# Q, K and V of a linear attention by seven products of halves in place of eight

## The chip, the cores and the metric

The kernel runs on one core of a Trainium2 chip. A core has TensorE (PE in the profile) for matrix products, VectorE (DVE), ScalarE (ACT) and GpSimd (POOL) for elementwise work, and SyncE (SP), which here only issues DMAs. Their common memory is SBUF, with 128 partitions; TensorE writes its sums to PSUM, eight banks of 128 x 512 numbers in 32 bits. The metric is the time of one execution on the device in microseconds (us), as the median of three runs.

## The reference

The input `x` is 4 blocks of 512 tokens with 512 features. Three layers follow, each with a layer norm in front and added to `x`: an FFN, an attention without softmax, and the same FFN again.

```python
def ffn(x, w_gate_up, w_proj):                 # w: ternary per group of 64
    gate, up = split(x @ ternary(w_gate_up).T) # 512 -> 2 x 2048
    h = silu(gate) * up
    return rms_norm(h) @ ternary(w_proj).T     # 2048 -> 512

def attention(x, w_qkv, w_proj, b_proj):       # 16 heads of 32
    q, k, v = relu(x @ wq.T), relu(x @ wk.T), x @ wv.T
    vk = [v, 1].T @ k                          # per head, 33 x 32
    out = vk @ q.T
    out = out[:-1] / (out[-1] + 1e-15)
    return out @ w_proj.T + b_proj

x = x + 0.5 * ffn(layernorm(x))
x = x + attention(layernorm(x))
x = x + 0.5 * ffn(layernorm(x))
```

## The kernel before

The tokens are cut into 16 tiles of 128 (tile i, quarter q; block b has four tiles). First the ternary FFN weights are made; then the tiles pass through the first FFN (`ffn_tile`, i from 0 to 15), the four blocks through attention, and the tiles again through the second FFN (i from 16 to 31). Each engine has its own instruction list in an order written out by hand, and semaphores are the only tie between the lists: `dve.wait_ge(rs_done, n)` holds VectorE's whole queue until the count is reached. An engine never takes a later instruction first.

An activation goes into a product as two numbers of 16 bits, a high and a low part (`x_high` is ScalarE's copy to 16 bits, `x_low` is VectorE's remainder). SyncE then turns both with a DMA transpose (`turn_x`, `turn_h`), since a product wants features on the partitions. Attention weights are cut the same way: w x = high high + high low + low high, three products for each 128 features.

In a tile of the FFN, TensorE makes for each quarter q eight products into a gate bank and eight into an up bank (`gate_up`, L1190), with two banks of each, so that quarter q+2 waits until quarter q has been read. ScalarE reads gate (`silu_gate`), VectorE multiplies with up (`hidden`, L884), ScalarE squares for the norm (`square`), and the tile before is scaled and cut (`h_high`, `h_low`, L897). After the four quarters `project` makes the 32 products of an older tile (`BEHIND` names it: 13 has tile 11, 14 has 12, 15 has 13, and 12 has both 9 and 10). `h_turned(i)` and `h_halves(i)` lie in a ring of eight slots, at i-2 and i-1.

In tiles 12 to 15 the sixteen units of attention weights (128 rows of w_qkv or w_proj) are cut, one at each quarter: `cut_high` on ScalarE (L757), its remainder on VectorE (L1074), `turn_unit` and `load_unit` on SyncE (L461 to L468). Two buffers (`aw_raw`) take turns.

In a block of attention `qkv(b, u)` (L1318) makes two banks for each u from 0 to 5: K for u 0 and 1, V for 2 and 3, Q for 4 and 5, with twelve products of 512 columns to a bank. ScalarE empties one of the two banks and VectorE the other. `keys_values` sums over tokens. Then for b > 0 come `project_attention(b-1, 0)`, `sums_by_queries(b)` (the denominators), `project_attention(b-1, 1..3)`, and `values_by_queries(b)`. Between the two by-queries steps ScalarE takes the logarithm and the exponential (L795, L799) as a guess of the inverse, and VectorE checks and mends it (`check_guess` L1094, `mend_guess` L1101); the checks also free the banks for the values. `att_out(b-1, t)` (L921, L924) adds a projection to `x` and so empties one of the two `proj_ps` banks; a projection waits until the one two uses before it has been taken. The layer norm and the turns of the next block run beside all this.

## Time and profile before

| | us |
|---|---|
| three runs | 882.1, 881.82, 881.25; median 881.82 |
| span of the profiled execution | 880.1 |

The profiled execution's own time is its span from the first to the last instruction; the runs' median is 1.7 us longer. In the profile TensorE is busy 98% of the span, VectorE 54%, ScalarE 45%, GpSimd 8%. Tiles 12 to 15 of the first FFN go from 261 to 351 us, attention from 351 to 535.5. A row of the timeline or the chain gives the start in us, then the length in us, the engine, the line and how many instructions were merged; what ended the idle time ahead of it stands in brackets. A product of 512 columns is shown with 379 ns, but they overlap: the next begins 216 ns later.

### The profile page before, as it was taken

Reading aid. Unit: us, or ns where it says so; the run is one execution under the profiler, and the core shown is the slowest. Engines: PE = TensorE matmul, PEld = TensorE weight load, DVE = VectorE, ACT = ScalarE, POOL = GpSimd, SP = SyncE. Lnnn points to the kernel's source line nnn. Section 1 sums busy time; section 2 is a strip of 40 time slices with the busy share of each in tenths; the row PEclk is TensorE's granted clock in tenths of the full one; section 3 lists DMA queues with packets and bytes.
Section 4 is the critical chain, followed back from the end, with each engine's and each line's share of the span. In section 5 each row is a group of like instructions: output and inputs, shape, how many; then the busy total and the mean of one; then the engine's idle time right before and its main releaser. Section 6 shows DMA issues by size and latency. Waiting matters only on the chain.

```text
span 880.1 us, 12730 instructions
## 1 busy us (share of the span) xinstructions
PE 863.7 (98%) x4836; PEld 404.0 (46%) x4902; DVE 478.1 (54%) x911; ACT 399.1 (45%) x762; POOL 71.3 (8%) x106
## 2 busy tenths in 40 slices
PE   6999999999999999999999999999999999999998
PEld 5544444444444444444444444444444444444445
DVE  7999997833335445518393938544334444333232
ACT  7976667555344445233333325343444434433331
POOL 2211001200000000100000000000000100000000
DMA  9998409985446677520203010063343334332336
GB/s 255 188 185 116 72 1 179 210 187 143 84 68 138 120 173 154 82 57 1 50 1 43 7 36 14 12 118 75 73 72 72 72 72 73 73 72 60 60 66 138
DMA packets 234829, 80.79 MB, mean 92 GB/s; under 512 B 221201, under 2 KB 224017, under 8 KB 234769
## 3 DMA queue, kind: packets, MB, share of 16 engines
q1 hardware_dynamic: 226944, 67.92, 40.8%
q0 software_dynamic: 3872, 4.72, 3.9%
q10 hardware_dynamic: 3952, 7.34, 2.5%
q8 instruction: 39, 0.64, 0.3%
q14 instruction: 22, 0.17, 0.1%
HBM read 25.43 MB, written 4.19 MB: 34 GB/s over the span
## 4 chain that ended last, share of the span: by engine, by line
PE 93%; DVE 3%; DMA 1%; issue 1%; ACT 1%; SPq 0%; DVEq 0%; ACTq 0%
PE proj_ps L1214 23%; PE gate_ps L1200 22%; PE up_ps L1200 22%; PE sum_ps L1337 5%; PE proj_ps L1237 5%; PE up_ps L1337 5%; PE gate_ps L1337 5%; PE proj_ps L1200 3%; PE gate_ps L1247 1%; DMA xs<-xn 1%; PE sum_ps L1186 1%; PE proj_ps L1350 1%; DMA xs<-in_L_attn_x_dram 1%; DVE stats L858 0%; PE gate_ps L1225 0%
## 5 line engine op out<-in xcount | busy, mean ns | idle before, releaser
L1214 PE MATMUL proj_ps<-down_w,slots 128*128 128x512 bf16 x909 | 202.7, 379 | 1.1 <-issue 0.2
L1200 PE MATMUL gate_ps<-gu_w,xT 128*128 128x512 bf16 (+1 forms) x878 | 199.8, 367 | 0.9
L1200 PE MATMUL up_ps<-gu_w,xT 128*128 128x512 bf16 (+1 forms) x878 | 199.7, 367 | 0.9
L884 DVE SCALAR_TENSOR_TENSOR slots<-up_ps,silu 128x512 f32<-128x512 f32 x117 | 80.9, 691 | 172.1 <-PE up_ps L1200 151.1
L631 ACT ACTIVATE silu<-gate_ps 128x512 f32<-128x512 f32 x117 | 69.0, 590 | 165.2 <-PE gate_ps L1200 165.1
L1214 PEld LDWEIGHTS proj_ps<-down_w,slots 128*128 128x128 f16 x928 | 90.7, 98 | 110.1 <-DVE xs L906 0.8
L1200 PEld LDWEIGHTS gate_ps<-gu_w,xT 128*128 128x128 f16 x896 | 85.5, 98 | 99.0
L1200 PEld LDWEIGHTS up_ps<-gu_w,xT 128*128 128x128 f16 x896 | 85.3, 98 | 98.2
L641 ACT ACTIVATE o_buf<-slots 128x512 f32<-128x512 f32 x128 | 80.4, 628 | 100.3 <-DVE slots L884 99.3
L897 DVE SCALAR_TENSOR_TENSOR slots<-slots,inv 128x512 f16<-128x512 f32 x124 | 91.1, 743 | 1.2 <-ACT slots L652 1.1
L906 DVE SCALAR_TENSOR_TENSOR xs<-proj_ps,xs 128x512 f32<-128x512 f32 x31 | 21.4, 691 | 126.3 <-PE proj_ps L1214 126.3
L652 ACT ACTIVATE slots<-slots,inv 128x512 f16<-128x512 f32 x124 | 86.5, 711 | 7.7 <-POOL inv L559 4.2
L554 POOL TENSOR_TENSOR rs<-ve,neg_half 128x1 f32<-128x1 f32 x48 | 39.7, 826 | 393.4 <-DVE ve L860 393.3
L559 POOL TENSOR_TENSOR inv<-ms,neg_half 128x1 f32<-128x1 f32 x32 | 18.8, 588 | 328.3 <-DVE ms L892 321.2
L1237 PE MATMUL proj_ps<-att_w,slots 128*128 128x512 f16 x192 | 42.6, 379 | 0.0
L618 ACT ACTIVATE xn<-lnx 128x512 f16<-128x512 f32 x44 | 27.6, 628 | 30.4 <-DVE lnx L867 30.3
L694 ACT ACTIVATE att_w<-sum_ps 128x1024 bf16<-128x1024 f32 x24 | 24.7, 1028 | 22.2 <-PE sum_ps L1186 21.7
L858 DVE BATCH_NORM_STATS2 stats<-xs 128x6 f32<-128x512 f32 x48 | 32.9, 685 | 2.1 <-DMA xs<-in_L_attn_x_dram 2.1
L1337 PE MATMUL up_ps<-att_w,xT 128*128 128x512 f16 x144 | 33.0, 379 | 0.0
L1337 PE MATMUL gate_ps<-att_w,xT 128*128 128x512 f16 x144 | 33.0, 379 | 0.0
L877 DVE TENSOR_TENSOR xn<-lnx,xn 128x512 f16<-128x512 f32 x44 | 30.1, 685 | 0.3
L1237 PEld LDWEIGHTS proj_ps<-att_w,slots 128*128 128x128 f16 x192 | 18.6, 98 | 24.4 <-DVE xs L921 2.5
(138 smaller groups left out, 773.4 us busy)
## 6 DMA issues: line engine op xcount, KB each, us to landing
out_dram<-xs SPq DMA_DIRECT2D x15, 256.0 KB, 2.4
xs<-in_L_attn_x_dram SPq DMA_DIRECT2D x3, 1024.0 KB, 7.3
aw_raw<-in_L_attn_w_qkv_dram ACTq DMA_DIRECT2D x12, 256.0 KB, 2.8
slots<-in_L_ffn_w_gate_up_dram ACTq DMA_DIRECT2D x5, 512.0 KB, 6.9
aw_raw<-in_L_attn_w_qkv_dram SPq DMA_DIRECT2D x8, 256.0 KB, 3.0
aw_raw<-in_L_ffn_w_gate_up_dram POOLq DMA_DIRECT2D x4, 256.0 KB, 4.9
aw_raw<-in_L_ffn_w_proj_dram POOLq DMA_DIRECT2D x4, 256.0 KB, 5.1
aw_raw<-in_L_attn_w_proj_dram ACTq DMA_DIRECT2D x4, 256.0 KB, 2.7
```

The lines of the kernel that those rows point to most:

```text
L554: nc.gpsimd.tensor_tensor(rs[:, t:t + 1], ve[:, t:t + 1], neg_half[:, :], ALU.pow).then_inc(rs_done, 1)
L631: nc.scalar.activation(silu_rows(j), bank(gate_ps, j), ACT.Silu, scale=gu_out(i))\
L641: nc.scalar.activation(junk, h_rows(i, q), ACT.Square, accum_out=ssq[:, i % 8, q:q + 1])\
L652: nc.scalar.activation(h_halves(i)[:, 0, q * 512:(q + 1) * 512], h_rows(i, q), ACT.Copy, scale=inv[:, i % 8:i % 8 + 1]).then_inc(hi_done, 1)
L858: step.done(nc.vector.bn_stats(out=stats[:, t, :], in_=x_tile(m % 4, t)))
L877: nc.vector.tensor_tensor(xn[:, t, 1, :], lnx[:, t % 2, :], xn[:, t, 0, :], ALU.subtract)\
L884: nc.vector.scalar_tensor_tensor(out=h_rows(i, q), in0=bank(up_ps, j), scalar=gu_out(i), in1=silu_rows(j), op0=ALU.mult, op1=ALU.mult).the ...
L897: nc.vector.scalar_tensor_tensor(out=h_halves(i)[:, 1, q * 512:(q + 1) * 512], in0=h_rows(i, q), scalar=inv[:, i % 8:i % 8 + 1], in1=h_hal ...
L1200: mm = nc.tensor.matmul(bank(ps, j)[:, first:first + width], xT(m)[:, t, r, k, :], gu_w[:, k, c:c + width], start=(k + r == 0), stop=(k == ...
L1214: mm = nc.tensor.matmul(proj_ps[:, use % 2, :], h_turned(i)[:, r, j, :], down_w[:, j, :], start=(r + j == 0), stop=(r == 1 and j == HC - 1))
L1237: mm = nc.tensor.matmul(proj_ps[:, use % 2, :], out_turned(b)[:, k, r, t * P:(t + 1) * P], att5[:, s, k, 12:16, :].rearrange("p u m -> p ( ...
L1337: mm = nc.tensor.matmul(dst, lhs, rhs, start=(m == 0), stop=(m == len(terms) - 1))
```

## The change

The product of an activation matrix and a weight matrix, each cut into halves along both sides, takes eight products of halves. The change takes seven (Strassen's scheme in Winograd's form), with sums of halves made on both sides.

- Weights: a pair of units (`pair_units(n)`, six pairs: four of K and V, two of Q) is loaded into `w_forms`, and `pair_sums` (VectorE, four steps of 256 columns) makes seven forms of 256 columns there, 1792 in all. `pair_high` (ScalarE) and `pair_low` (VectorE) cut them in two steps of 896 columns each, and `turn_pair` turns both parts. There is one `w_forms`: `load_pair(n+1)` waits for `pair_low(n)`. This runs in tiles 12 to 14. The four units of w_proj follow in tile 15 and block 0.
- Activations: for tiles s and s+2 of a block `spread` (ScalarE) writes the normed rows, `forms_sums` (VectorE, four steps of 256), `forms_high` and `forms_low` (two steps of 896 each) and `turn_forms` follow. For block 0 they run in tiles 13 to 15, for the others one block ahead.
- Products: `product(b, s, p)` for s = 0, 1 makes K and V of two pairs of tiles with six products of 512 columns, for s = 2 Q with twelve of 256. Their order is the table `PRODUCTS`. Three banks gather each s; `part` copies what stands in a bank midway, `summed` adds such a copy to another bank, `positive` takes the relu.
- Places: K, V, Q and the copies lie where the gate and up weights lay. `keep_weights` writes these to DRAM in tiles 8 to 11 (GpSimd's queue, four times 1 MB), and `bring_weights` reads them back from the end of `keys_values(3)` on.
- Order: the outputs of block b-1 (`output`, `output_low`) now run in block b; `att_out(b-1, 1)` stands behind the four `check_guess`; the four projections of block 3 stand behind quarter 1 of tile 16, not behind quarter 3.

SyncE's queue from the turn of tile 12's hidden rows on (`slots<-slots`, 16 squares) into tile 14, before. `att_w<-aw_hl` and `att_w<-bias` are turns of one unit, `aw_raw<-in_L_attn_w_qkv_dram` its load.

```order
L455 DMA_TRANSPOSE slots<-slots 128x16x128 [waits hi_done,hT_here1,hT_here0]
L455 DMA_TRANSPOSE slots<-slots 128x16x128 [waits lo_done]
L435 DMA_TRANSPOSE xT<-xn 128x8x128 [waits up_done,xn_done]
L468 DMA_TRANSPOSE att_w<-aw_hl 128x8x128 [waits awlo_done]
L464 DMA aw_raw<-in_L_attn_w_qkv_dram 128x512
L468 DMA_TRANSPOSE att_w<-bias 128x8x128 [waits awlo_done]
L464 DMA aw_raw<-in_L_attn_w_qkv_dram 128x512
L468 DMA_TRANSPOSE att_w<-aw_hl 128x8x128 [waits awlo_done]
L464 DMA aw_raw<-in_L_attn_w_proj_dram 128x512
```

The same place after. `att_w<-slots` with 14 squares is `turn_pair`, `aw<-in_L_attn_w_qkv_dram` is `load_pair`, in eight pieces of 32 rows where Q is loaded.

```order
L567 DMA_TRANSPOSE slots<-slots 128x16x128 [waits hi_done,hT_here1,hT_here0]
L567 DMA_TRANSPOSE slots<-slots 128x16x128 [waits lo_done]
L589 DMA_TRANSPOSE att_w<-slots 128x14x128 [waits whigh_done]
L589 DMA_TRANSPOSE att_w<-slots 128x14x128 [waits wlow_done]
L579 DMA aw<-in_L_attn_w_qkv_dram 32x512 [waits wlow_done]
L579 DMA aw<-in_L_attn_w_qkv_dram 32x512 x7
L589 DMA_TRANSPOSE slots<-slots 128x14x128 [waits whigh_done,proj_done]
L589 DMA_TRANSPOSE slots<-slots 128x14x128 [waits wlow_done]
```

In place of a turn of 8 squares and one load in turns, two turns of 14 squares stand ahead of eight loads, and the loads of a pair wait for the cut of the pair before.

VectorE's queue from the end of tile 13 (`ffn_out`, `xs<-proj_ps,xs`) through the first quarter of tile 14, before. L884 is `hidden`, L897 is `h_low`, L1074 cuts a weight unit.

```order
L906 SCALAR_TENSOR_TENSOR xs<-proj_ps,xs 128x512 [waits proj_done]
L884 SCALAR_TENSOR_TENSOR slots<-up_ps,silu 128x512 [waits gate_used,up_done]
L858 BN_STATS stats<-xs 128x6 [waits proj_used]
L859 BN_AGGR mv<-stats 128x2 [waits v_step]
L860 TENSOR_SCALAR ve<-mv 128x1 [waits v_step]
L897 SCALAR_TENSOR_TENSOR slots<-slots,inv 128x512 [waits hi_done]
L1074 SCALAR_TENSOR_TENSOR aw_hl<-aw_raw,r_unit,aw_hl 128x512 [waits awhi_done]
L884 SCALAR_TENSOR_TENSOR slots<-up_ps,silu 128x512 [waits gate_used,up_done]
```

The same place after. L1168 is `hidden`, L1181 `h_low`, L1371 `pair_sums`, L1343 `turn_shift`, L1378 `pair_low`.

```order
L1190 SCALAR_TENSOR_TENSOR xs<-proj_ps,xs 128x512 [waits proj_done]
L1168 SCALAR_TENSOR_TENSOR slots<-up_ps,silu 128x512 [waits pairT_here,gate_used,up_done]
L1181 SCALAR_TENSOR_TENSOR slots<-slots,inv 128x512 [waits hi_done]
L1371 TENSOR_TENSOR aw<-aw 128x256 [waits raw_here]
L1371 TENSOR_TENSOR aw<-aw 128x256
L1371 TENSOR_TENSOR aw<-aw 128x256 [waits wsum_done] x2
L1343 SCALAR_TENSOR_TENSOR few<-few 128x1 [waits rs_done] x2
L1168 SCALAR_TENSOR_TENSOR slots<-up_ps,silu 128x512 [waits gate_used,up_done]
L1181 SCALAR_TENSOR_TENSOR slots<-slots,inv 128x512 [waits hi_done]
L1378 SCALAR_TENSOR_TENSOR slots<-aw,r_unit,slots 128x896 [waits whigh_done] x2
```

Between the hidden products of quarters 0 and 1 now stands a wait for loaded weights (`raw_here`), and `turn_shift`, for which ScalarE's `spread` waits.

VectorE's queue at the end of block 1, before. `xs<-proj_ps,y_scale,xs` with the row behind it is `att_out(0, t)`, L1094 the checks, L1101 the mends.

```order
L921 SCALAR_TENSOR_TENSOR xs<-proj_ps,y_scale,xs 128x512 [waits proj_done,bias_here]
L924 TENSOR_TENSOR xs<-xs,bias 128x512 [waits proj_used]
L921 SCALAR_TENSOR_TENSOR xs<-proj_ps,y_scale,xs 128x512 [waits proj_done]
L924 TENSOR_TENSOR xs<-xs,bias 128x512 [waits proj_used]
L1094 SCALAR_TENSOR_TENSOR slots<-gate_ps,den_eps,silu 128x512 [waits guess_done]
L1094 SCALAR_TENSOR_TENSOR slots<-up_ps,den_eps,silu 128x512 [waits guess_done]
L1094 SCALAR_TENSOR_TENSOR slots<-gate_ps,den_eps,aw_raw 128x512 [waits guess_done]
L1094 SCALAR_TENSOR_TENSOR aw_hl<-up_ps,den_eps,aw_raw 128x512 [waits guess_done]
L1101 SCALAR_TENSOR_TENSOR silu<-slots,silu 128x512 [waits gate_used]
L1101 SCALAR_TENSOR_TENSOR silu<-slots,silu 128x512 [waits up_used]
L1101 SCALAR_TENSOR_TENSOR aw_raw<-slots,aw_raw 128x512 [waits gate_used]
L1101 SCALAR_TENSOR_TENSOR aw_raw<-aw_hl,aw_raw 128x512 [waits up_used]
```

The same place after. L1205 and L1208 are `att_out`, L1444 the checks, L1450 the mends.

```order
L1205 SCALAR_TENSOR_TENSOR xs<-proj_ps,few,xs 128x512 [waits proj_done,bias_here]
L1208 TENSOR_TENSOR xs<-xs,aw 128x512 [waits proj_used]
L1444 SCALAR_TENSOR_TENSOR gu_w<-gate_ps,few,silu 128x512 [waits guess_done]
L1444 SCALAR_TENSOR_TENSOR gu_w<-up_ps,few,silu 128x512 [waits guess_done]
L1444 SCALAR_TENSOR_TENSOR gu_w<-gate_ps,few,aw 128x512 [waits guess_done]
L1444 SCALAR_TENSOR_TENSOR aw<-up_ps,few,aw 128x512 [waits guess_done]
L1205 SCALAR_TENSOR_TENSOR xs<-proj_ps,few,xs 128x512 [waits proj_done]
L1208 TENSOR_TENSOR xs<-xs,aw 128x512 [waits proj_used]
L1450 SCALAR_TENSOR_TENSOR silu<-gu_w,silu 128x512 [waits check_done] x2
L1450 SCALAR_TENSOR_TENSOR aw<-gu_w,aw 128x512 [waits check_done]
L1450 SCALAR_TENSOR_TENSOR aw<-aw 128x512 [waits check_done]
```

The second `att_out` stood ahead of the checks, which wait for ScalarE's guess, and now stands behind them.

```diff
+FORMS = 7
+WIDE = FORMS * HALF
+SPAN = WIDE // 2
+WEIGHT_PAIRS = 6
...
+PRODUCTS = ((0, 1), (0, 2), (0, 6), (0, 7), (0, 5), (1, 1), (0, 3), (0, 4), (1, 2), (1, 6), (1, 7), (1, 5), (2, 1),
+            (1, 3), (1, 4), (2, 2), (2, 6), (2, 7), (2, 5), (2, 3), (2, 4))
...
+def pairs_cut(i):
+    return range(2 * (i - 12), 2 * (i - 12) + 2) if 12 <= i < LAYER - 1 else range(0)
...
+            def load_pair(n):
+                if n:
+                    sp.wait_ge(wlow_done, 2 * n)
...
+            def turn_pair(n):
+                if n >= DC:
+                    sp.wait_ge(proj_done, FFN_USE[n + 6] + 1)
+                for r, done in enumerate((whigh_done, wlow_done)):
+                    sp.wait_ge(done, 2 * n + 2)
+                    place = kv_w[:, r, :, :, n * P:(n + 1) * P] if n < DC else q_w[:, n - DC, r, :, :, :]
+                    sp.dma_start_transpose(place.rearrange("p o k m -> p (o k) m"), w_cut(n)[:, r, :])\
+                      .then_inc(pairT_here, 16)
...
-                for u in units_cut(i):
-                    if u == 0:
-                        sp.wait_ge(abs_done, UNITS)
-                        load_unit(0)
-                        load_unit(1)
-                    turn_unit(u)
-                    if u + 2 < UNITS:
-                        load_unit(u + 2)
+                if i == 12:
+                    load_pair(0)
+                for n in pairs_cut(i)[:1]:
+                    turn_pair(n)
+                    load_pair(n + 1)
+                if i == LAYER - 1:
+                    turn_forms(4, 0)
                 if i > EARLY:
                     turn_h(i - 1)
...
+            def keep_weights(q):
+                pool.wait_ge(wq_done, PIECES)
+                nc.gpsimd.dma_start(gu_kept[:, q, :], gu_w[:, q, :, :, :].rearrange("p s k f -> p (s k f)"))\
+                  .then_inc(gu_saved, 16)
...
+            def pair_high(n):
+                act.wait_ge(wsum_done, DC * (n + 1))
...
+                    nc.scalar.activation(w_cut(n)[:, 0, cols], w_forms[:, cols], ACT.Copy, scale=r_unit[:, 0:1])\
+                      .then_inc(whigh_done, 1)
...
+                for k, t in enumerate((s + 2, s)):
+                    act.wait_ge(shift_done, place_of(m - 4, 0) + PAIRED.index(t) + 1)
+                    nc.scalar.activation(x_forms[:, k * D:(k + 1) * D], x_tile(m % 4, t), ACT.Identity,
+                                         scale=rs[:, t:t + 1], bias=shift[:, t:t + 1]).then_inc(spread_done, 1)
...
+                    if q % 2:
+                        for n in pairs_cut(i)[q // 2:q // 2 + 1]:
+                            pair_high(n)
+                    if (i, q) in ((13, 0), (14, 0)):
+                        spread(4, i - 13)
...
+                if i in (14, 15) and q == 0:
+                    dve.wait_ge(pairT_here, 64 if i == 14 else 32 * WEIGHT_PAIRS)
...
+            def pair_sums(n):
+                dve.wait_ge(raw_here, 16 * pair_loads(n))
+                for k, (a, c, to) in enumerate(((0, 2, 4), (1, 0, 0), (1, 4, 5), (3, 5, 6))):
+                    if k >= 2:
+                        dve.wait_ge(wsum_done, 4 * n + (1, 3)[k - 2])
+                    nc.vector.tensor_tensor(quarter_of(w_forms, to), quarter_of(w_forms, a), quarter_of(w_forms, c),
+                                            ALU.subtract).then_inc(wsum_done, 1)
...
+                for n in pairs_cut(i)[q // 2:q // 2 + 1]:
+                    if q % 2:
+                        pair_low(n)
+                    else:
+                        pair_sums(n)
...
+                if (i, q) in ((12, 3), (14, 0)):
+                    for t in (0, 2) if i == 12 else (1, 3):
+                        turn_shift(4, t)
+                if (i, q) in ((13, 1), (14, 2)):
+                    forms_sums(4, i - 13)
...
+                for h in range(HPG):
+                    check_guess(b, h)
+                if b:
+                    att_out(b - 1, 1)
+                for h in range(HPG):
+                    mend_guess(b, h)
...
-                for u in range(5):
-                    qkv(b, u)
+                for s, p in PRODUCTS[:-2]:
+                    product(b, s, p)
                 keys_values(b)
-                qkv(b, 5)
+                for s, p in PRODUCTS[-2:]:
+                    product(b, s, p)
```

## Rows read from the trace of the kernel before

**Rows 1.** The page: span, and busy time of TensorE.

```profile
span 880.1 us, 12730 instructions
...
PE 863.7 (98%) x4836; PEld 404.0 (46%) x4902; DVE 478.1 (54%) x911; ACT 399.1 (45%) x762; POOL 71.3 (8%) x106
```

**Rows 2.** Stages: span, busy PE PEld DVE ACT POOL, clock, DMA share, GB/s.

```profile
268.00:351.00 83.00, 82.58 (x379) 37.61 (x385) 41.99 (x77) 42.12 (x83) 5.15 (x7) 1.00 0.73 148
...
400.00:445.00 45.00, 45.00 (x393) 20.22 (x384) 26.57 (x50) 15.32 (x24) 2.95 (x4) 1.00 0.13 25
```

**Rows 3.** The chain of waits, block 1 of attention: start us, us, what.

```profile
413.12 2.59 PE up_ps L1337 x12
...
426.07 1.23 PE proj_ps L1350 x117
...
436.25 7.88 PE proj_ps L1237 x36
```

**Rows 4.** The chain of waits, the last product, which is in 256-column halves.

```profile
870.53 3.49 PE proj_ps L1225 x32
```

**Rows 5.** Groups by line and shape: count, busy us, mean ns, idle before.

```profile
L877 DVE TENSOR_TENSOR xn<-lnx,xn 128x512 f16<-128x512 f32 x44 | 30.1, 685 | 0.3
...
L694 ACT ACTIVATE att_w<-sum_ps 128x1024 bf16<-128x1024 f32 x24 | 24.7, 1028 | 22.2 <-PE sum_ps L1186 21.7 <-DVE att_w L948 0.5
...
L757 ACT ACTIVATE bias<-aw_raw,r_unit 128x512 f16<-128x512 f32 x8 | 5.7, 716 | 2.3 <-DMA aw_raw<-in_L_attn_w_qkv_dram 1.6 <-DMA aw_raw<-in_L_attn_w_proj_dram 0.6
...
L914 DVE SCALAR_TENSOR_TENSOR xs<-proj_ps,xs 128x256 f32<-128x256 f32 x1 | 0.4, 424 | 2.8 <-PE proj_ps L1225 2.8
```

**Rows 6.** Timeline of block 1, ScalarE and VectorE: start, us, engine, line.

```profile
436.39 0.69 ACT L795 ACTIVATE silu<-gate_ps,den_eps 128x512 f32<-128x512 f32 x1 [4.46 <-PE gate_ps L1247]
...
438.98 0.75 DVE L921 SCALAR_TENSOR_TENSOR xs<-proj_ps,y_scale,xs 128x512 f32<-128x512 f32 x1 [2.21 <-PE proj_ps L1237]
...
440.78 0.75 DVE L1094 SCALAR_TENSOR_TENSOR slots<-gate_ps,den_eps,silu 128x512 f32<-128x512 f32 x1 [0.32 <-ACT silu L799]
...
443.42 1.29 DVE L1101 SCALAR_TENSOR_TENSOR silu<-slots,silu 128x512 f32<-128x512 f32 x2
```

**Rows 7.** Timeline of SyncE's queue, tiles 12 and 13.

```profile
274.42 1.97 SPq L461 DMA_DIRECT2D aw_raw<-in_L_attn_w_qkv_dram  x4
276.43 1.23 SPq L468 DMA_TRANSPOSE att_w<-aw_hl  x1
277.70 0.58 SPq L464 DMA_DIRECT2D aw_raw<-in_L_attn_w_qkv_dram  x1
...
306.81 5.10 SPq L455 DMA_TRANSPOSE slots<-slots  x2
```

**Rows 8.** Timeline, start of tile 13.

```profile
288.79 1.89 PE L1200 MATMUL gate_ps<-gu_w,xT 128*128 128x512 bf16 x8
...
292.45 0.69 DVE L884 SCALAR_TENSOR_TENSOR slots<-up_ps,silu 128x512 f32<-128x512 f32 x1 [2.76 <-PE up_ps L1200]
```

**Rows 9.** One stretch of the second FFN with turns only.

```profile
609.00:615.00 6.00, 5.95 (x28) 2.74 (x28) 0.78 (x3) 0.57 (x2) 0.55 (x1) 1.00 1.14 212
```

**Rows 10.** DMA issues: out<-in, queue, count, KB each, median us to landing.

```profile
xs<-in_L_attn_x_dram SPq DMA_DIRECT2D x3, 1024.0 KB, 7.3
...
aw_raw<-in_L_attn_w_qkv_dram SPq DMA_DIRECT2D x8, 256.0 KB, 3.0
...
aw_raw<-in_L_attn_w_qkv_dram SPq DMA_DIRECT2D x16, 64.0 KB, 2.0
...
slots<-slots SPq DMA_TRANSPOSE x60, 4.8
...
xT<-xn SPq DMA_TRANSPOSE x44, 3.4
```

**Rows 11.** Timeline, TensorE's longest idle time, and that stretch's clock.

```profile
51.37 1.90 PE L1200 MATMUL gate_ps<-gu_w,xs 128*128 128x512 bf16 x8 [1.69 <-DMA xs<-xn]
...
50.00:55.00 5.00, 3.58 (x16) 1.67 (x18) 4.83 (x9) 0.70 (x3) 0.81 (x2) 1.00 0.90 135
```

More of the change, by code:

```diff
@@ new lines, in earlier_high, with ahead @@
+            def earlier_high(b, h):
+                if b:
+                    output_high(b - 1, h)
+                else:
+                    h_high(LAYER - 1, h)
+            def ahead(b, s, what):
+                if b < BLOCKS - 1:
+                    if what == "spread":
+                        spread(5 + b, s)
+                    else:
+                        for half in range(2):
+                            forms_high(5 + b, s, half)
+                else:
+                    for t in (2 * s, 2 * s + 1):
+                        if what == "forms":
+                            x_high(8, t)
@@ new lines, in pair_low @@
+            def pair_low(n):
+                for half in range(2):
+                    cols = slice(half * SPAN, half * SPAN + SPAN)
+                    dve.wait_ge(whigh_done, 2 * n + half + 1)
+                    nc.vector.scalar_tensor_tensor(out=w_cut(n)[:, 1, cols], in0=w_forms[:, cols],
+                                                   scalar=r_unit[:, 0:1], in1=w_cut(n)[:, 0, cols], op0=ALU.mult,
+                                                   op1=ALU.subtract).then_inc(wlow_done, 1)
```

712 lines of the change are left out of this document (501 added, 211 removed).

## The prediction

> **What bounds the kernel now.** I read the page's busy times first: TensorE works 98% of an 880.1 us span [rows 1]. The granted clock is 1.00 in every stretch, and in a block of attention TensorE is busy all 45.00 us, while VectorE has 26.57 and ScalarE 15.32 [rows 2]. The chain of waits through block 1 of attention is products end to end: 2.59 us for twelve 512-column ones (0.216 each), 1.23 for keys times values, 7.88 for three of the four output projections [rows 3]. So a product taken away is worth its 0.216 us, as long as no other engine becomes late. The second thing to see is where that can happen: in the last four tiles of the first FFN (12 to 15) TensorE has 82.58 of 83.00 us, but the DMA engines are already busy for 0.73 of the time [rows 2], because SyncE loads and turns the attention weights there.
>
> **The products.** Before, Q, K and V take twelve groups of twelve products a block: 144 x 0.216 = 31.1 us. After, K and V take 2 x 7 x 6 = 84 products of 512 columns, Q takes 2 x 7 x 6 = 84 of 256. The 256-column product is in the trace: 32 in 3.49 us, 0.109 each [rows 4], so its weight load stays hidden. 84 x 0.216 + 84 x 0.109 = 27.3 us: 3.9 us less a block, 15.5 in four. If 256 columns cost as much as 512, Q alone would take 9 us more a block and the edit would lose; the row excludes that.
>
> **Evictions, sums and cuts in a block.** VectorE now has 9 sums from PSUM, 4 statistics, 8 half-width sums, 4 cuts of 896 columns, 4 output products, 4 lows, 4 checks, 4 mends and 4 output additions of two steps. With 0.685 for 512 columns, 0.425 for 256 [rows 5], some 0.07 less each back to back, and 0.685 + 1.5 x 0.26 = 1.07 for 896, that is about 33.5 us of a block of some 43. ScalarE gets about 27 us. Both fit, so the question is order. I laid the two queues beside 21 products of 1.295 us each. The copy "one" is ready some 0.4 us before the second product that adds to its bank, "two" and "four" 0.4 to 0.5 before theirs. In block 2 an att_out (1.4 us) and in block 0 the two unit_low stand ahead of sums_ahead(b, 0), and summed c22 of the second pair of tiles is then 0.5 us late for product 4: 0.5 in each of these blocks. The turned forms of the next block are there 6 us early (low cut done 31 us into the block, turn about 4.5).
>
> **The wait that the new order makes.** In block 1 the sums by queries end at 436.25 and ScalarE starts its logarithms at 436.39; the first check starts at 440.78 and the mends at 443.42 [rows 3, 6]. Before, att_out(b-1, 1) stands ahead of the checks and runs at 438.98. Now it stands behind all four. TensorE's fourth projection uses the bank that it empties: due 436.25 + 2 x 2.59 = 441.43, and the bank is free at 443.42 + 0.75 = 444.17. That is 2.7 us of idle TensorE in each of blocks 1 to 3, 8.1 in all (the work before it in the block shifts both sides alike). VectorE's checks cannot be earlier, since they wait for ScalarE's chain. Nothing hides it: the values by queries stand behind that projection. Block 0 has no such projection.
> Attention: 15.5 - 8.1 - 1.0 - 0.3 (the second turned forms of block 0, which may be turned only after project(13)) = 6.1 us gained. Bounds: 15.5 if none of the waits comes, 3 if VectorE is 1 us late in every block.
>
> **The tail of the first FFN.** This is the costly place. Six pairs of weight slices go one after another through one buffer (w_forms): load, pair_sums (VectorE), pair_high (ScalarE), pair_low (VectorE), two turns (SyncE), and the next load waits for pair_low. Before, two units alternate in two buffers and each load has a whole quarter of a tile.
> Prices: pair_sums four 256-column steps, two of them waiting for the one before, 1.5 us. pair_high 2 x (0.716 + 0.33) less the overlap, 2.05; pair_low ends 1.1 after it [rows 5]. A turn of 8 squares is issued in 1.23 us, two of 16 in 5.10 [rows 7], so one of 14 in about 2.0. Two loads of 256 KB land 0.6 + 3.0 us after the first is issued; eight of 64 KB take 2 x 1.97 to issue and the last lands 2.0 after its start, together 5.4 [rows 7, 10].
> On the clock of the trace, with tile 13 starting at 288.79 and its first hidden at 292.45 [rows 8]:
> (steps of 512 columns on VectorE and ScalarE are taken at 0.6 to 0.8, the statistics of a tile at 1.1, a step of 512 and two short ones.) Pair 2: sums from 293.8, square(13,1) ends 297.55, high 299.6, low 300.7. Turns and loads: 300.7 + 0.35 + 2.0 + 3.6 = 306.6. Pair 3: sums to 308.1, statistics 1.1, hidden(13,3) 0.65, square 0.8, so high 310.7 to 312.75 and low 313.85. On VectorE then statistics, forms_low (2.0), mean_squares and ffn_out, to 318.0.
> Tile 14 starts at 309.51, the earliest it can. hidden(14,0) comes at 318.0 to 318.65 in place of 313.1, and up of quarter 2 (due 318.15) waits 0.5. Then VectorE stands in pair_sums(4): SyncE turns pair 3 until 317.0, so the eight loads land at 322.4. Behind it in VectorE's queue are turn_shift and hidden(14,1); behind spread(4,1), which needs the shift, ScalarE has silu(14,1). 322.4 + 1.5 + 0.3 + 1.4 + 0.6 = 326.3, and TensorE has wanted that gate bank since 320.4: 5.9 us.
> Pair 4: hidden, square, high 329.85, low 330.95; turns to 334.1; loads land 339.5. Pair 5: sums 341.05, forms_sums 342.75, hidden(14,3) 343.4. TensorE, in tile 15 since 336.65 (rest of tile 14 until 329.75, then project(12), 32 x 0.216), waits for it 1.6 us, and 1.8 more for silu(15,0) behind pair_high(5) (346.3). hidden(15,0) may write its slot only when all pairs are turned: turn_h(13) ends at 346.6, the two turns of pair 5 are issued until 350.55 and land at about 353.1 (4.5 after issue, between 3.4 for 8 squares by the same view and 4.8 for 16 [rows 10]). up(15,2) starts at 353.8 in place of 348.7: 5.1 us; 0.4 more for silu(15,1).
> 0.5 + 5.9 + 1.6 + 1.8 + 5.1 + 0.4 = 15.3 us of idle TensorE. TensorE bounds everything behind it, so nothing gives it back. Bounds: if an 896-column step cost what a 512-column one costs, 1.0 us less in each of three rounds, and landings were 1 us quicker, 9 us. If each load also queued behind its own pair's turns (two of 14 squares are 0.92 MB, 4.3 us at the 212 GB/s at which turns run with a DMA share of 1.14 [rows 9]), 4.3 more in three rounds, 28 us. I take 15.3, which uses the landing times of rows in the same stretch.
>
> **The weights that leave.** 4 MB go out during tiles 8 to 11 and come back from keys_values of block 3 on. Loads of 1 MB land in 7.3 us [rows 10]. Quarters 0 and 1 have some 17 us before they are used, quarters 2 and 3 another 17, since the four projections of block 3 now stand behind quarter 1. I take 0; if GpSimd's transfers are half as quick, 0 to 5 us would show at the start of the second FFN.
>
> **Sum.** 880.1 - 6.1 + 15.3 = 889.3 for the profiled execution; the runs' median is 1.7 us above its span: 891.0 us.
>
> **The rule that speaks against.** The longest idle time of TensorE in this trace is 1.69 us, and the clock is 1.00 after it [rows 11]; the forecast makes gaps of 5 to 6 us. If the clock then fell to its lower level of 1.2 GHz, products would take twice as long for a while. After the 5.9 us gap that is covered by later waits; after the last one the three remaining products of tile 15 (1.73 each) would double, 5.2 us: 896. The Trainium skill (TensorE: Matmul & The Clock Gate, Part 1: The HAM clock gate) says in our words that the array goes to the lower clock when it has been idle and returns after being kept busy; no row here shows an idle time long enough to tell.
>
> **Rivals and chances.**
> Forecast (0.50): 891, own range 885 to 897.
> The tail keeps pace (0.19): the six pairs cost TensorE 0 to 4 us, because some wait on my path ends sooner, above all the loads of pairs 4 and 5. For it: in the rows before, each load lands in 2 to 3 us and ScalarE and VectorE are half idle. Against it: the load waits for pair_low and for two turns, and VectorE itself stands in the wait. Then 881.8 - 6.1 + 0 to 4 = 876 to 880, faster. It decides when pair 4's rows land before about 316.5 in place of 322.4.
> Attention gives all 15.5 while the tail costs 15.3 (0.06): 881.6, no change. For it only that the 2.7 us wait rests on one bank; against it the credits leave no third bank.
> The clock (0.11): 896.
> The DMA engines (0.14): before they are at 0.73, now a tile turns 11,264 columns in place of 9,216, and loads queue behind turns: 15.3 + 8 to 13, so 899 to 904.
> That the products don't shrink as said is excluded by rows 4.
> A measurement of this kernel tells about 0.2% (1.8 us) from no change. Faster: the second case and a hundredth of the forecast, 0.20. Same 0.05. Slower 0.75. The range 877 to 900 leaves out part of the second case, some 0.08, and about 0.12 at the top.
>
> **What would show it.** In the profile after: block 0 of attention starts near 366, not 351; TensorE idle 5 to 6 us in tile 14, ended by ScalarE's silu, with VectorE waiting for a DMA of the attention weights at pair_sums; a second gap in tile 15 ended by the hidden product. Blocks 1 to 3 last 43.9 to 44.4 us with a gap of 2.7 us ended by att_out. Products of Q at 0.109. No gap at the weights that come back. The forecast is wrong if TensorE stays dense through tiles 14 and 15, or if blocks take 41.3.

## The result, and the profile of the changed kernel

| | before | after |
|---|---|---|
| median, us | 881.82 | 901.32 |
| runs | 881.25 to 882.1 (3) | 897.92 to 904.52 (4) |
| span of the profiled execution, us | 880.1 | 897.5 (its time 899.47) |
| ratio, 95% interval | | 1.022 [1.021, 1.024] |

The change makes the kernel 2.2% slower. The forecast was 891.0 with a range up to 900, so its sign is right and its size half of what came.

The page of the changed kernel, the lines that answer to [rows 1], with the clock by slices:

```profile
span 897.5 us, 13199 instructions
...
PE 861.2 (96%) x4998; PEld 414.1 (46%) x4998; DVE 511.9 (57%) x979; ACT 442.1 (49%) x822; POOL 72.2 (8%) x114
...
PEclk9999999999999978999999999999999999999999
```

TensorE is busy 861.2 us against 863.7, though the change takes some 15 us of products away. Slower products, in the slices where the clock reads 7 and 8 and in block 1, are 6.5 us of the difference (5.1 and 1.4, see below). The rest can't be read from these two numbers: the profile before has 4836 products beside 4902 weight loads, so records are missing there, and the one after has 4998 of both. By stages (span, busy PE PEld DVE ACT POOL, clock, DMA share, GB/s): tiles 14 and 15, the four blocks of attention, and the start of the second FFN.

```profile
309.52:370.70 61.18, 47.56 (x195) 19.87 (x193) 32.32 (x58) 26.09 (x47) 3.52 (x5) 0.86 0.68 132
370.70:415.90 45.20, 44.90 (x425) 23.99 (x424) 27.14 (x58) 26.26 (x40) 2.19 (x4) 1.00 0.65 128
415.90:462.60 46.70, 43.11 (x419) 22.73 (x409) 32.73 (x63) 25.29 (x39) 2.19 (x4) 0.96 0.25 40
462.60:506.90 44.30, 41.61 (x418) 22.36 (x410) 33.33 (x63) 25.45 (x39) 2.19 (x4) 1.00 0.26 43
506.90:551.10 44.20, 41.51 (x416) 22.43 (x409) 30.44 (x55) 22.81 (x37) 3.47 (x6) 1.00 0.30 73
```

Attention starts at 370.7 and ends at 551.1, where before it ran from 351 to 535.5. That splits the 17.4 us between the two spans: +19.7 up to the start of attention, -4.1 in it, +1.8 behind it.

TensorE in tiles 14 and 15 (timeline: start, length, engine, line, in brackets the idle time and what ended it). Before, the same groups followed one another every 1.73 us.

```profile
319.60 1.90 PE L1622 MATMUL up_ps<-gu_w,xT 128*128 128x512 bf16 x8 [0.97 <-DVE slots L1168]
328.86 3.60 PE L1622 MATMUL gate_ps<-gu_w,xT 128*128 128x512 bf16 x8 [7.36 <-ACT silu L804]
332.25 2.76 PE L1622 MATMUL up_ps<-gu_w,xT 128*128 128x512 bf16 x8
334.85 7.07 PE L1636 MATMUL proj_ps<-down_w,slots 128*128 128x512 bf16 x32
...
348.94 1.90 PE L1622 MATMUL gate_ps<-gu_w,xT 128*128 128x512 bf16 x8
356.01 3.59 PE L1622 MATMUL up_ps<-gu_w,xT 128*128 128x512 bf16 x8 [5.17 <-DVE slots L1168]
359.40 2.84 PE L1622 MATMUL gate_ps<-gu_w,xT 128*128 128x512 bf16 x8
362.07 1.89 PE L1622 MATMUL up_ps<-gu_w,xT 128*128 128x512 bf16 x8
```

Two long gaps, where they were forecast. What was not in the sum stands behind each of them: eight products take 3.39 us (328.86 to 332.25) and then 2.60, in place of 1.73 each. That is 5.1 us of slower products in both places together. The granted clock falls within the idle time and is 0.50 over the eight products, which is the lower of its two levels (1.2 of 2.4 GHz). The stretches are the gap, the products behind it, and those behind the second gap; TensorE had stood idle for 7.36 us in the first and for 5.17 in the second.

```profile
322.00:328.00 6.00, 0.00 (x0) 0.00 (x0) 1.66 (x6) 1.19 (x2) 0.00 (x0) 0.65 0.21 55
328.00:332.00 4.00, 3.14 (x8) 1.20 (x9) 2.03 (x3) 3.78 (x7) 0.00 (x0) 0.50 0.00 0
...
356.00:360.00 4.00, 3.99 (x10) 1.49 (x11) 2.62 (x4) 3.78 (x9) 0.00 (x0) 0.50 1.17 247
```

VectorE in the same tiles: L1371 is `pair_sums`, with its wait for loaded rows.

```profile
325.01 1.56 DVE L1371 TENSOR_TENSOR aw<-aw 128x256 f32<-128x256 f32 x4 [4.50 <-DMA aw<-in_L_attn_w_qkv_dram]
326.49 0.22 DVE L1343 SCALAR_TENSOR_TENSOR few<-few 128x1 f32<-128x1 f32 x2
328.91 0.69 DVE L1168 SCALAR_TENSOR_TENSOR slots<-up_ps,silu 128x512 f32<-128x512 f32 x1 [2.19 <-ACT silu L804]
...
342.04 1.55 DVE L1371 TENSOR_TENSOR aw<-aw 128x256 f32<-128x256 f32 x4 [7.24 <-DMA aw<-in_L_attn_w_qkv_dram]
...
355.26 0.69 DVE L1168 SCALAR_TENSOR_TENSOR slots<-up_ps,silu 128x512 f32<-128x512 f32 x1 [4.69 <-DMA slots<-slots]
```

And SyncE's queue there, which answers to [rows 7]: turns of tile 12's hidden rows, turns of pair 3, loads of pair 4, turns of pair 4, loads of pair 5, turns of tile 13's hidden rows, turns of pair 5.

```profile
307.09 6.06 SPq L567 DMA_TRANSPOSE slots<-slots  x2
313.80 5.69 SPq L589 DMA_TRANSPOSE att_w<-slots  x2
319.53 3.84 SPq L579 DMA_DIRECT2D aw<-in_L_attn_w_qkv_dram  x8
332.29 3.51 SPq L589 DMA_TRANSPOSE slots<-slots  x2
335.84 4.54 SPq L579 DMA_DIRECT2D aw<-in_L_attn_w_qkv_dram  x8
340.49 7.82 SPq L567 DMA_TRANSPOSE slots<-slots  x2
348.47 3.93 SPq L589 DMA_TRANSPOSE slots<-slots  x2
```

The mechanism is the one described: load, sums, cut, turn, next load, one after another. Each station is later than forecast: the rows of pair 4 are there at 325.0 and not 322.4, `hidden(15, 0)` runs at 355.3 and not 353.1.

In attention, the three waits for `att_out(b-1, 1)` and a small one at the start of block 1; TensorE again:

```profile
419.57 1.47 PE L1771 MATMUL sum_ps<-att_w,slots 128*128 128x512 f16 x6 [0.90 <-ACT gu_w L1023]
...
457.42 4.16 PE L1661 MATMUL proj_ps<-xT,slots 128*128 128x512 f16 x12 [2.69 <-DVE xs L1205]
...
503.11 2.76 PE L1661 MATMUL proj_ps<-xT,slots 128*128 128x512 f16 x12 [2.69 <-DVE xs L1205]
...
562.21 4.06 PE L1661 MATMUL proj_ps<-xT,slots 128*128 128x512 f16 x18 [1.45 <-DVE xs L1205]
```

The wait is 2.69 us each time, as forecast (2.7). In block 1 the twelve products behind it take 4.16 us in place of 2.76: the clock fell there too. The last row is one that the forecast didn't have: the third projection of block 3 waits 1.45 us for `att_out(2, 3)`, which stands behind `hidden(16, 1)`.

### The profile page after: what moved, and what is told of

Its sections match the earlier page's. It is cut to its first block, busy times and chain, and to the rows that moved or that the text cites. A ratio compares the mean times of both kernels' runs of the same rounds, so it can differ in the third digit from the quotient of the medians.

```text
span 897.5 us, 13199 instructions
## 1 busy us (share of the span) xinstructions
PE 861.2 (96%) x4998; PEld 414.1 (46%) x4998; DVE 511.9 (57%) x979; ACT 442.1 (49%) x822; POOL 72.2 (8%) x114
## 4 chain that ended last, share of the span: by engine, by line
PE 76%; DVE 8%; DMA 5%; SPq 4%; ACT 4%; issue 2%; ACTq 0%; POOL 0%; DVEq 0%; POOLq 0%
PE proj_ps L1636 19%; PE up_ps L1622 18%; PE gate_ps L1622 18%; DMA aw<-in_L_attn_w_qkv_dram 3%; PE gate_ps L1771 3%; PE proj_ps L1622 3%; PE sum_ps L1774 3%; PE proj_ps L1661 3%; PE sum_ps L1771 3%; SPq L589 3%; PE up_ps L1771 2%; PE gate_ps L1774 1%; DVE aw L1371 1%; DVE slots L1168 1%; DVE gu_w L1444 1%
## 5 line engine op out<-in xcount | busy, mean ns | idle before, releaser
L1168 DVE SCALAR_TENSOR_TENSOR slots<-up_ps,silu 128x512 f32<-128x512 f32 x117 | 80.8, 690 | 180.0 <-PE up_ps L1622 133.5
L1622 PE MATMUL gate_ps<-gu_w,xT 128*128 128x512 bf16 (+1 forms) x776 | 175.7, 370 | 7.7 <-ACT silu L804 7.6
L1622 PE MATMUL up_ps<-gu_w,xT 128*128 128x512 bf16 (+1 forms) x776 | 175.7, 370 | 6.1 <-DVE slots L1168 6.1
L1181 DVE SCALAR_TENSOR_TENSOR slots<-slots,inv 128x512 f16<-128x512 f32 x124 | 91.1, 743 | 3.1 <-ACT slots L825 3.0
L699 POOL TENSOR_TENSOR few<-few 128x1 f32<-128x1 f32 x48 | 35.6, 743 | 356.8 <-DVE few L1138 356.8
L1661 PE MATMUL proj_ps<-xT,slots 128*128 128x512 f16 x192 | 44.7, 388 | 9.5 <-DVE xs L1205 9.5
L704 POOL TENSOR_TENSOR inv<-ms,few 128x1 f32<-128x1 f32 x32 | 18.9, 590 | 355.9 <-DVE ms L1176 349.2
L1771 PE MATMUL gate_ps<-att_w,slots 128*128 128x512 f16 x144 | 35.0, 379 | 0.0
L1661 PEld LDWEIGHTS proj_ps<-xT,slots 128*128 128x128 f16 x192 | 18.5, 99 | 35.4 <-DVE xs L1205 14.0
L1771 PE MATMUL sum_ps<-att_w,slots 128*128 128x512 f16 x120 | 28.1, 379 | 0.9 <-ACT gu_w L1023 0.9
L1774 PE MATMUL sum_ps<-slots 128*128 128x256 f16 x240 | 28.8, 273 | 0.0
L1622 PE MATMUL gate_ps<-gu_w,att_w 128*128 128x512 bf16 x120 | 28.3, 379 | 0.0
```

The lines of the kernel that those rows point to most:

```text
L699: nc.gpsimd.tensor_tensor(rs[:, t:t + 1], ve[:, t:t + 1], neg_half[:, :], ALU.pow).then_inc(rs_done, 1)
L1168: nc.vector.scalar_tensor_tensor(out=h_rows(i, q), in0=bank(up_ps, j), scalar=gu_out(i), in1=silu_rows(j), op0=ALU.mult, op1=ALU.mult).the ...
L1181: nc.vector.scalar_tensor_tensor(out=h_halves(i)[:, 1, q * 512:(q + 1) * 512], in0=h_rows(i, q), scalar=inv[:, i % 8:i % 8 + 1], in1=h_hal ...
L1622: mm = nc.tensor.matmul(bank(ps, j)[:, first:first + width], xT(m)[:, t, r, k, :], gu_w[:, q, side, k, first:first + width], start=(k + r ...
L1661: mm = nc.tensor.matmul(proj_ps[:, use % 2, :], out_turned(b)[:, k, r, t * P:(t + 1) * P], proj_w[:, s, k, :], start=(m == 0), stop=(m == ...
L1771: mm = nc.tensor.matmul(gathered(s, where), x_turned(b)[:, s, r, o, k, :], kv_w[:, v, w, k, :], start=begin, stop=(m == len(terms) - 1), s ...
```

## The experiments

Twelve kernels ran, each four to twelve times, beside the kernel before (881.4 to 881.5 us). Each is the changed kernel with the edits named, and "less" and "more" are differences of medians. The changed kernel's own four runs lie 6.6 us apart, and the interval of its median is 1.6 us to either side: a difference to it of less than some 2 us says nothing. Two theories stood against each other. One: the loss of the tail is a chain of latencies through one buffer, and its order can be mended. The other: the DMA engines or the clock set the time.

**att_out(b-1, 1) ahead of the checks**

```diff
+                if b:
+                    att_out(b - 1, 1)
                 for h in range(HPG):
                     check_guess(b, h)
-                if b:
-                    att_out(b - 1, 1)
```

> The changed kernel with one order undone: att_out(b-1, 1) ahead of the four checks again. In the changed kernel's trace TensorE idles 2.69 us ahead of project_attention(b-1, 3) in each of blocks 1 to 3, ended by att_out, and in block 1 the twelve products behind it take 3.9 us in place of 2.6. Theory (the wait is due to that order alone): the three gaps vanish, blocks 1 to 3 take 41.3 to 41.6 us, 8.1 us less and 1.3 of slow products: 892 to 893 us in place of 901.3. Rival (the checks are the real bound, and the values by queries then wait for them): less than 2 us gained, and a gap of over 2 us ahead of the values.

Measured: 891.1 us, 1.010 [1.009, 1.012], 10.2 less than the changed kernel. The three gaps are gone, and blocks 2 and 3 take 41.4 and 41.3 us against 45.1 before the change: 3.8 us a block, which is what the products come to (31.1 less 27.3). So the seven products give what they should. 3 x 2.69 is 8.1, the slower products of block 1 are 1.4 more, and 0.7 is within the spread of the runs.

**turn_shift of block 0's last tiles ahead of pair_sums(4)**

```diff
+                if (i, q) == (14, 0):
+                    for t in (1, 3):
+                        turn_shift(4, t)
                 for n in pairs_cut(i)[q // 2:q // 2 + 1]:
```

> The changed kernel with turn_shift(4, 1) and (4, 3) ahead of pair_sums(4) in VectorE's queue, so that ScalarE's spread(4, 1) and silu(14, 1) don't wait for loaded weights. Theory (the 7.36 us gap in tile 14 is VectorE's wait for the loads of pair 4, passed on through the shift): gate of quarter 3 starts at about 322.5 in place of 328.86, its up waits for hidden(14, 1) until about 327, and the chain of pairs comes 2 us sooner, so hidden(15, 0) at about 353 in place of 355.3; whole time 2 to 3 us less, 898 to 899. Rival (only the shift matters and the pairs are not the chain): the whole 7 us come back, 894.

Measured: 897.6, 1.018 [1.017, 1.020], 3.7 less. The gap of 7.36 us shrinks to 1.31, but the next quarter waits 2.64, and attention starts at 368.1 (2.6 sooner). Most of the gap was only passed on to the next instruction that waits for the same chain.

**Each pair's loads between the two turns of the pair before**

```diff
                 for r, done in enumerate((whigh_done, wlow_done)):
                     sp.wait_ge(done, 2 * n + 2)
+                    if r and n + 1 < WEIGHT_PAIRS:
+                        load_pair(n + 1)
```

> The changed kernel, but SyncE issues the loads of pair n+1 right after the low cut of pair n, ahead of the turn of pair n's low part (2.3 to 2.9 us of issue) and not behind it. Theory (latency chain through one buffer: cut, turn, load, sums): pairs 3, 4 and 5 each come 2 to 3 us sooner, hidden(15, 0) at 348 to 350 in place of 355.3, attention starts 5 to 8 us sooner, 893 to 896 us. Rival (the DMA engines are the bound in tiles 12 to 15, share 0.94 in tile 14's start): the loads share the engines with the turns, sums come at most 1 us sooner, under 2 us gained.

Measured: 893.3, 1.013 [1.011, 1.014], 8.0 less; attention starts at 364.8.

```profile
321.32 1.56 DVE L1370 TENSOR_TENSOR aw<-aw 128x256 f32<-128x256 f32 x4 [2.55 <-DMA aw<-in_L_attn_w_qkv_dram]
...
336.09 1.55 DVE L1370 TENSOR_TENSOR aw<-aw 128x256 f32<-128x256 f32 x4 [4.99 <-DMA aw<-in_L_attn_w_qkv_dram]
```

The same bytes go the same way, and the rows are there 3.7 and 6.0 us sooner. The rival of the DMA engines falls: they don't hold the loads, the order of the queue does.

**The clock held by idle products**: 24, 20 and 10 products into `sum_ps`, whose results nobody reads, at the places of the three falls

```diff
+                    if (i, q, side) in ((14, 3, 0), (15, 2, 1)):
+                        keep_warm(24 if i == 14 else 20)
```

> The changed kernel with products that nobody reads put into three kinds of gaps, each shorter than the gap: 24 of 512 columns (5.2 us) ahead of gate(14, 3), 20 (4.3 us) ahead of up(15, 2), 10 (2.2 us) ahead of each project_attention(b-1, 3). Nothing else is changed. Theory (after an idle time the clock falls to 1.2 GHz and products take twice as long: eight took 3.39 us, not 1.73, after each of the two long gaps): the granted clock is 1.00 throughout, the slow products vanish, 2.6 us less in tile 15 and 1.3 in block 1; the slow ones of tile 14 were covered by a later wait. 896 to 898 us, and the runs lie closer together than 898 to 904.5. Rival (the clock falls for another reason, or the slow products are the memory's): no change, or slower by what fillers add.

Measured: 901.05, 1.022 [1.021, 1.023], no change: the 896 to 898 expected didn't come. TensorE's tail and its stretch:

```profile
329.69 1.90 PE L1628 MATMUL gate_ps<-gu_w,xT 128*128 128x512 bf16 x8 [2.21 <-ACT silu L804]
...
357.10 1.90 PE L1628 MATMUL up_ps<-gu_w,xT 128*128 128x512 bf16 x8 [1.20 <-DVE slots L1168]
359.76 1.90 PE L1628 MATMUL gate_ps<-gu_w,xT 128*128 128x512 bf16 x8 [0.77 <-ACT silu L804]
...
309.80:370.13 60.33, 52.62 (x240) 22.90 (x239) 32.79 (x60) 25.50 (x46) 3.24 (x5) 1.00 0.67 127
```

The clock is 1.00 over the whole stretch, against 0.86, and the slow products are gone, so it is the idle time that lets it fall. From the last gap's end to attention it is now 13.0 us (357.10 to 370.13) and was 14.7 (356.01 to 370.70), so the fall costs 1.7 us there, not the 2.6 by which the products are longer: the next gate group has to wait 0.77 us for silu (2.66 us after the group before, 357.10 to 359.76). Those 1.7 us don't reach the end of the kernel. The chain of pairs runs 0.8 to 1.1 us later in this execution, and block 0 takes 47.8 us and not 45.2, with new waits of 1.30 us for the turned second forms and 0.97 for a copy. Whether the added products caused that isn't shown. What the run does show: with the clock held the kernel is as slow as without, to within some 2 us, so the falls are not what parts 901 from 882.

**The first three moves together**

> The three changes of order together: att_out(b-1, 1) ahead of the checks, turn_shift(4, 1) and (4, 3) ahead of pair_sums(4), and each pair's loads issued between its two turns. Theory (the tail's loss is a chain of latencies through one buffer, and attention's is one order on VectorE): the first gave 10.2 us, the second 3.7, the third 8.0. The first is independent of the others; the second and the third take from the same wait of gate(14, 3), so together 9 to 10 and not 11.7: 901.3 - 10.2 - 9.5 = about 881.6, no change from before, with attention starting near 361. Rival (each change only moves the wait, which comes back in the next round): attention starts at 364 or later and the time is 886 or more.

Measured: 880.03, 0.999 [0.998, 1.000], 1.6 less than forecast. Attention starts at 359.7, 11.0 sooner. The three moves of order give back the whole loss; what stays is this:

```profile
339.02 1.90 PE L1624 MATMUL gate_ps<-gu_w,xT 128*128 128x512 bf16 x8 [1.20 <-ACT silu L803]
346.03 3.45 PE L1624 MATMUL up_ps<-gu_w,xT 128*128 128x512 bf16 x8 [5.11 <-DVE slots L1167]
```

**The same with a place of its own for the sixth pair's cut**, so that `hidden(15, 0)` waits for five pairs; the sixth is turned in four pieces of seven squares

```diff
-                    dve.wait_ge(pairT_here, 64 if i == 14 else 32 * WEIGHT_PAIRS)
+                    dve.wait_ge(pairT_here, 64 if i == 14 else 32 * (WEIGHT_PAIRS - 1))
```

> As the three together, and the halves of the sixth pair are cut into a place of their own (the end of att_w, o_buf and the end of slot 1), so hidden(15, 0) waits for the turns of the fifth pair and not of the sixth. Theory (the last gap, at up(15, 2), is hidden(15, 0) waiting for the landing of the last turns): it goes, with the slow products behind it: 4 to 6 us less than the three together, about 876, attention starts near 356. Rival (another wait stands close behind: the silu of tile 15 behind pair_high(5)): 1 to 2 us less.

Measured: 882.13, 1.002 [1.000, 1.004]: nothing gained, 2.1 us more. The wait of `hidden(15, 0)` is gone, and another stands two groups later. TensorE, and ScalarE before it:

```profile
341.33 1.90 PE L1641 MATMUL up_ps<-gu_w,xT 128*128 128x512 bf16 x8 [0.39 <-DVE slots L1184]
349.22 3.60 PE L1641 MATMUL gate_ps<-gu_w,xT 128*128 128x512 bf16 x8 [5.99 <-ACT silu L820]
```

```profile
347.96 0.72 ACT L946 ACTIVATE aw<-aw,r_unit 128x512 f16<-128x512 f32 x1 [5.88 <-DMA aw<-in_L_attn_w_proj_dram]
348.59 0.58 ACT L820 ACTIVATE silu<-gate_ps 128x512 f32<-128x512 f32 x1
```

ScalarE stands in the cut of the first projection slice, whose load is issued behind the turns of the sixth pair, and the silu is queued behind it. The rival that I had named (a silu behind `pair_high(5)`) is the wrong one; the kind was right.

**Q's rows in two DMAs of 256 KB**, together with all the above and `att_out(2, 3)` ahead of `hidden(16, 1)`, and, below, alone in the changed kernel

```diff
-                        for h in range(HPG):
-                            sp.dma_start(rows[h * HEAD:h * HEAD + HEAD, :], q_v[u, h]).then_inc(raw_here, 16)
+                        sp.dma_start(rows, w_qkv[0:D].rearrange("(h u e) d -> u h e d", h=HPG, u=DC)[u]).then_inc(raw_here, 16)
```

> As before this, and Q's rows of a pair loaded by two DMAs of 256 KB in place of eight of 64 KB, and att_out(2, 3) ahead of hidden(16, 1). Theory: the eight loads took 5.4 us against 3.6, on the chain of pairs 4 and 5, of which some 1 to 2 us still show; the addition ahead of hidden(16, 1) gives 1.4: 2 to 3 us less than the run with its own place for the last cut, about 873, faster than the kernel before by 1%. Rival: nothing waits for the loads any more, 1.4 less.

Measured: 885.9, 1.005 [1.004, 1.006], 3.8 more than the run before it, although `att_out(2, 3)` was moved as well.

> The changed kernel with one edit: the rows of Q of a pair come in two DMAs of 256 KB in place of eight of 64 KB, the same bytes. Theory (latency and issue of the loads on the chain): raw rows of pair 4 land 1.8 us sooner and those of pair 5 3.6 sooner, so the wait of gate(14, 3) is 5.5 in place of 7.4 and attention starts near 367: 897.5 to 898.5. Rival (the DMA engines' bytes bound the loads): same landing times, 901.

Measured: 904.7, 1.027 [1.025, 1.029], 3.4 more than the changed kernel. Both expectations fail. The loads are issued quicker (1.32 us for two) and land far later: SyncE, then the rows' first use, then a stretch in which SyncE has issued nothing behind these two loads (DMA share and GB/s are its last columns).

```profile
322.30 1.32 SPq L577 DMA_DIRECT2D aw<-in_L_attn_w_qkv_dram  x2
```

```profile
331.51 1.56 DVE L1369 TENSOR_TENSOR aw<-aw 128x256 f32<-128x256 f32 x4 [8.18 <-DMA aw<-in_L_attn_w_qkv_dram]
```

```profile
326.00:331.00 5.00, 0.00 (x0) 0.00 (x0) 0.00 (x0) 0.00 (x0) 0.00 (x0) 0.56 0.24 94
```

The source is 4 x 32 x 512, the destination 128 x 512. It takes 9.2 us from issue to use against 5.5 for the eight small ones, at 94 GB/s with 0.24 of the DMA engines busy: about 4 of 16. It holds up what comes behind it too: with the second such pair of loads just ahead, the two turns of tile 13's hidden rows take 13.76 us to issue, against 7.82 behind eight small ones.

```profile
344.22 13.76 SPq L567 DMA_TRANSPOSE slots<-slots  x2
```

The Trainium skill (DMA: Bandwidth & Descriptors, Why a DMA increments its semaphore by 16 and not by 1) says that a DMA is spread over the largest number of engines, up to 16, that divides the outermost dimension of both sides. For 4 x 32 rows that is 4, and the trace agrees (0.24 of 16); for 32 rows it is 16, which no stretch here shows by itself.

**The cuts of the projection slices a quarter later**, with a place of its own for the last cut, eight small loads and `att_out(2, 3)` moved

```diff
-                    if i == LAYER - 1 and q < 2:
-                        unit_high(12 + q)
+                    if i == LAYER - 1 and q in (1, 2):
+                        unit_high(11 + q)
```

> As the run with its own place for the last cut (without the two-DMA loads of Q), and the cuts of the first two projection slices stand one quarter of tile 15 later on ScalarE and VectorE, so that silu(15, 1) isn't behind a load that lands at 348; att_out(2, 3) stands ahead of hidden(16, 1). Theory (the wait of 5.99 us that took the place of hidden(15, 0)'s is ScalarE standing in that cut): it goes, attention starts near 354 in place of 362.5, some 2 us come back at the second turned forms of block 0, and 1.4 us go at the start of the second FFN: about 874.5. Rival (the next wait stands close behind again, such as the turns of x's forms): attention's first twelve products are held, 878 or more, no better than the three changes of order by more than the 1.4.

Measured: 880.3, 0.999 [0.998, 1.000]. Tile 15 has waits of 1.20 and 0.39 us left and attention starts at 355.5, near the 354 expected. Then

```profile
363.66 2.74 PE L1791 MATMUL sum_ps<-att_w,slots 128*128 128x512 f16 x6 [5.43 <-ACT att_w L1039]
```

the third group of products waits 5.43 us for a copy by ScalarE, which is still in the work of tile 15. It has stood 4.16 us for the first projection slice again, 1.41 for a turn of x's forms, and last this, right ahead of the copy:

```profile
362.40 0.72 ACT L841 ACTIVATE slots<-slots,inv 128x512 f16<-128x512 f32 x1 [3.48 <-POOL inv L720]
```

That is `h_high` of tile 15, which waits for the norm's factor (`inv`, GpSimd); VectorE gets to the sum for it at 361.40, behind `forms_low` and a slice's remainder. The rival holds.

**The three moves and att_out(2, 3) ahead of hidden(16, 1)**

> The three changes of order together, and att_out(2, 3) ahead of hidden(16, 1) in the first tile of the second FFN. Theory (TensorE's third projection of block 3 waits 1.45 us for the bank that att_out(2, 3) empties): 1.4 us less than the three alone, 878.6. Rival: another wait of the same tile takes its place, 880.

Measured: 878.95, 0.9965 [0.995, 0.998], 1.1 less than the three alone; the projection's wait is 0.23 us, and was 1.71 there.

**The loads of the projection slices between the last pair's turns, the cut of x's second forms behind silu(15, 3)**

```diff
                     if n == WEIGHT_PAIRS - 1:
+                        if r:
+                            load_unit(12)
+                            load_unit(13)
```

> As the run with the cuts of the projection slices one quarter later, and two more moves: the loads of the first two projection slices are issued between the turns of the sixth pair's two halves (about 342 in place of 346.4), and ScalarE cuts the second forms of x behind silu(15, 3) and not ahead of it. Theory (the 5.43 us in the first products of attention are ScalarE's and VectorE's work of tile 15, held first by a load and then by the turned forms): attention starts near 355 with a wait of 1 to 2 us for the second forms: 875 to 876. Rival (the queue of turns on SyncE is full by now: whatever is taken out of one place stands in the next): 879 to 880 again.

Measured: 876.17, 0.994 [0.993, 0.995]. This version beats both kernels, by 5.2 us (0.6%) and 25 us. TensorE's waits around the start of attention are these:

```profile
340.93 1.90 PE L1642 MATMUL gate_ps<-gu_w,xT 128*128 128x512 bf16 x8 [1.20 <-ACT silu L820]
343.22 1.90 PE L1642 MATMUL up_ps<-gu_w,xT 128*128 128x512 bf16 x8 [0.38 <-DVE slots L1184]
...
360.75 1.47 PE L1791 MATMUL sum_ps<-att_w,slots 128*128 128x512 f16 x6 [2.68 <-ACT att_w L1039]
```

The 2.68 us that are left end with the same copy, again behind `h_high` of tile 15, which stood 2.87 us for `inv`.

**Without the loads of pairs 3 to 5**, with the two moves of att_out alone. The last of the four pairs of keys and values and both pairs of Q are left out, so this kernel computes something else; it is there for its time alone

```diff
-                for side, u in enumerate(pair_units(n)):
+                for side, u in enumerate(pair_units(n) if n < 3 else ()):
```

> The changed kernel with att_out(b-1, 1) ahead of the checks and att_out(2, 3) ahead of hidden(16, 1); the rows of pairs 3, 4 and 5 are not loaded (the last key and value slices and all of Q are made from what lies in the buffer). Everything else, turns too, stays. Theory (load, sums, cut and turn one after another hold tiles 14 and 15; the loads are 5.4 us of each round of some 17): the waits of tile 14 go, a part of that at hidden(15, 0) stays, attention starts at 353 to 356 and the time is 872 to 876. Rival (the turns alone hold the tail, the loads only lie beside them): attention starts after 360, 880 or more.

Measured: 873.45, 0.991 [0.989, 0.992]; attention starts at 354.8. The two moves of att_out alone would stand at about 890 (an estimate, 891.1 less the 1.1), so the loads in the chain are worth some 16 us. The stretch from 309.8 to there:

```profile
309.80:354.80 45.00, 43.27 (x197) 19.15 (x199) 30.43 (x54) 25.49 (x46) 2.69 (x4) 1.00 0.80 151
```

Every turn is still made, the DMA engines are busier than in the changed kernel (0.80 against 0.68), and the tail is nearly dense. So the turns alone don't hold it; the chain does, with the loads in it. The best version above is 2.7 us from this one. That is no bound, since this one lacks the two moves of order in the tail.

## Why the prediction was right in sign and wrong in size

**The products** (15.5 us): right, but for a slip: 31.1 less 27.3 is 3.8 a block and 15.2 in four, not 3.9 and 15.5. The run without the waits measured 3.8; twelve half-width products take 1.31 us.

**The wait of att_out(b-1, 1)** (3 x 2.7 = 8.1): right, 2.69 three times, shown by its removal. Attention as a whole gave 4.1 us, not 6.1; it is the second term that missed. By blocks against before: -3.8, +1.6, -0.8, -1.0. The difference is block 1, forecast at -1.2: 0.90 for a copy that is late at its start, 1.4 of slower products behind the wait, and 0.5 that I didn't trace.

**The tail of the first FFN** (15.3): this is the step that failed. It measured 19.7. The stations were named rightly, and the idle time is even below the sum (0.97 + 7.36 + 5.17 = 13.5). Two things were mis-sized. The chain of pairs is 2.2 us longer at its end (355.3 against 353.1), and what the sum had too short is SyncE's issuing. The two turns of pair 3, priced at 2.0 each (the rows for 8 and 16 squares give 2.2), take 5.69 us right behind the turns of the tile before; the eight loads of pair 5 take 4.54 in place of 3.9, and the turns of hidden rows right behind them 7.82 in place of 5.10. And I priced slower products only as a rival. Those of tile 14 cost nothing, as that passage says, since the waits of 1.6 and 1.8 us forecast behind them shrank to 0.3. From `hidden(15, 0)` to attention it was 15.4 us where the forecast has 13.2: 2.2 more, of which 1.7 is the clock, by the run that holds it, and the rest a wait for silu. 15.3 + 2.2 + 2.2 = 19.7. The rival of the DMA engines, which came nearest in time (899 to 904), had the wrong cause: with the same bytes and the loads issued earlier, the rows came 3.7 and 6.0 us sooner.

**Nothing behind attention** (0): 1.8 us. I had seen that the four projections of block 3 moved behind quarter 1, and looked only at the weights that come back (these cost nothing, as forecast), not at what `att_out(2, 3)` stands behind. The chip gave 1.1 of it back when it was moved.

**The median above the span** (1.7): 3.8, since the profiled execution (899.47) is one of the quicker ones. 2.0 + 4.4 + 1.8 + 2.1 is the 10.3 us by which the forecast missed: the tail is the largest part and less than half.

What stays open is why the changed kernel's runs lie 6.6 us apart, where those before lie within 1. With the clock held they lie within 2.6, but the three moves in order, with one fall left, still spread over 4.6. The changed kernel's mean clock goes with its time (0.990 in the run of 897.92, 0.985 in that of 904.52); longer gaps would give the same, so which comes first isn't shown.
